# Attention and a mixture of experts on one core: the first expert's outputs, the overflow lists and their loads in another order

## The reference

```python
scores = jax.nn.softmax(x @ gate_w.T, axis=-1)
topk_w, topk_idx = jax.lax.top_k(scores, TOP_K)          # TOP_K = 6
...                                                      # C = 768 slots per expert, in order of token
g = jnp.einsum('ecd,efd->ecf', buf, w_gate)              # F = 176
u = jnp.einsum('ecd,efd->ecf', buf, w_up)
eo = jnp.einsum('ecf,edf->ecd', jax.nn.silu(g) * u, w_down)
y = jnp.zeros_like(x).at[st].add(gathered)               # gathered: eo times the token's weight
return y + _shared_swiglu(hidden_states, sh_gate, sh_up, sh_down)
```

## Time and profile before

| | |
|---|---|
| median of 3 runs | 2354.23 us (2347.09 to 2356.7) |
| the profiled execution's own time | 2333.68 us |
| its span in the profile | 2331.8 us, 38661 instructions |
| mean granted clock of TensorE | 0.978 of full speed |
| busy, PE, DVE, ACT, POOL | 2200.4, 1329.0, 1201.2, 817.6 us |
| chain that ended last | PE 84%, DVE 8%, ACT 3%, issue 3%, POOL 2%, DMA 1% |
| POOL at line 2104 | 264 instructions, 413.6 us |

### The profile page before, as it was taken

How to read it: one execution, slowest core, us unless ns; L and a number is a source line. 1 busy time by engine, 2 the same in 40 slices (tenths; PEclk the granted TensorE clock), 3 DMA queues, 4 the chain that set the end, 5 groups by cost and what they waited for, 6 DMA issues and landing times.

```text
span 2331.8 us, 38661 instructions
## 1 busy us (share of the span) xinstructions
PE 2200.4 (94%) x14776; PEld 1986.8 (85%) x14776; DVE 1329.0 (57%) x2870; ACT 1201.2 (52%) x2231; POOL 817.6 (35%) x791
## 2 busy tenths in 40 slices
PE   8999999999999999999999999998798999999970
PEld 7999998998989899898989989898687888888860
DVE  4444444545554454555545455555667887888853
ACT  4544444444444454444445444444445777777753
POOL 3111112000014400002440000261345888878785
PEclk9999999999999999999999999999899999999995
DMA  5866722122113212111322211141549988888856
GB/s 191 318 266 263 287 80 62 47 66 75 50 54 119 89 57 77 53 51 59 120 84 60 77 59 44 60 141 46 179 160 297 212 205 206 203 204 204 211 61 231
DMA packets 152705, 310.61 MB, mean 133 GB/s; under 512 B 26529, under 2 KB 88225, under 8 KB 152513
## 3 DMA queue, kind: packets, MB, share of 16 engines
q1 hardware_dynamic: 103888, 251.98, 32.1%
q0 software_dynamic: 48192, 55.68, 12.4%
q10 hardware_dynamic: 432, 0.40, 0.1%
HBM read 168.01 MB, written 149.34 MB: 136 GB/s over the span
## 4 chain that ended last, share of the span: by engine, by line
PE 84%; DVE 8%; ACT 3%; issue 3%; POOL 2%; DMA 1%; ACTq 0%; POOLq 0%; SPq 0%; DVEq 0%
PE bank L841 52%; PE bank L1201 20%; PE bank L851 7%; PE bank L1304 2%; PE bank L1214 2%; DVE ub L1705 1%; POOL y_part L2104 1%; DVE stats L2019 0%; DVE bank L1889 0%; DVE bank L1886 0%; ACT q_hi L1429 0%; ACT silu_b L1505 0%; POOL slots L2094 0%; DVE xe_lo L1956 0%; DVE ha_lo L1891 0%
## 5 line engine op out<-in xcount | busy, mean ns | idle before, releaser
L1201 PEld LDWEIGHTS bank<-v,a 128*128 128x128 f32 x4608 | 604.2, 191 | 44.1 <-ACT a L1453 0.8
L1201 PE MATMUL bank<-v,a 128*128 128x129 f32 x4608 | 617.4, 275 | 0.6 <-ACT a L1453 0.6
L2104 POOL DMA_INDIRECT y_part<-y_e,row_token x264 | 413.6, 1567 | 104.2 <-issue 84.3
L2074 POOL TENSOR_TENSOR decay_all<-decay_all,tab 128x128 f32<-128x128 f32 x128 | 60.6, 473 | 944.7 <-DMA decay_all<-decay_dram 944.4
L1449 ACT ACTIVATE a<-bank,c_s 128x512 f32<-128x512 f32 x384 | 263.0, 686 | 181.4 <-PE bank L841 167.9
L1453 ACT ACTIVATE a<-ub 128x512 f32<-128x512 f32 (+1 forms) x256 | 133.9, 524 | 379.0 <-DVE ub L1705 371.9
L2094 POOL DMA_INDIRECT slots<-rows,slot_u x192 | 189.4, 987 | 275.7 <-PE bank L1201 119.4
L841 PE MATMUL bank<-q_hi,k_hi 128*128 128x512 f32 (+1 forms) x640 | 262.5, 410 | 11.3 <-DVE ub L1705 9.6
L1684 DVE TENSOR_TENSOR q_lo<-bank,q_hi 128x512 fp32r<-128x512 f32 x128 | 88.4, 691 | 278.1 <-ACT q_hi L1429 278.1
L841 PE MATMUL bank<-q_lo,k_hi 128*128 128x512 f32 (+1 forms) x640 | 237.9, 372 | 0.0
L841 PE MATMUL bank<-q_hi,k_lo 128*128 128x512 f32 (+1 forms) x640 | 236.9, 370 | 0.0
(11 more groups left out here) (216 smaller groups left out, 4911.5 us busy)
## 6 DMA issues: line engine op xcount, KB each, us to landing
slots<-acc SPq DMA_DIRECT2D x65, 816.0 KB, 7.8
w_raw_f<-in_wffn SPq DMA_DIRECT2D x66, 624.0 KB, 5.3
xr<-slots SPq DMA_DIRECT2D x64, 544.0 KB, 5.4
decay_all<-decay_dram SPq DMA_DIRECT2D x128, 128.0 KB, 3.2
w_hi<-w_dram SPq DMA_DIRECT2D x24, 384.0 KB, 4.4
w_lo<-w_dram SPq DMA_DIRECT2D x24, 384.0 KB, 5.0
sum<-y_part SPq DMA_DIRECT2D x16, 512.0 KB, 10.6
wc_hi<-wc_dram SPq DMA_DIRECT2D x24, 256.0 KB, 2.8
```

The costliest lines, as they stand in the source:

```text
L1201: ins = e.matmul(dst[:, tt, r, :], a32[u % NA][:, r, t0:t0 + P], v[n % 3][:, s, :], start=(s == 0 and r == 0), stop=(s == 2 * g + tt), ski ...
L2074: e.tensor_tensor(arg[:, GROUP:GROUP + P], arg[:, P:GROUP], mask, ALU.add)
L2104: e.indirect_dma_start(out=y_part[part], out_offset=bass.IndirectOffsetOnAxis(ap=token, axis=0), in_=y_e[y][:, j, :], in_offset=None, boun ...
```

## The change

It has three parts, none of which changes what is computed.

1. At place 1 of the expert loop, both pairs of `down` of expert 0 stand directly in front of `gate_up(k, 1)`, behind the first third of expert 1's `gate_up`, the turn of expert 2 and the rounding of expert 3's weights. Before, they stood behind `gate_up(k, 2)`. At all other places `down` stays where it was.
2. `counted` and `jobs(0)` follow `hidden` of step 11, which is the first step with no routing work in front of it; before, they followed the whole shared stage.
3. The task `over_in`, which gathered rows and weights job by job, is split in `over_rows` and `over_weights`. All eight row gathers come first, and they no longer wait for the last `gate_up` of the shared stage; the four weight gathers still do, since their buffers lie over shared inputs.

```diff
--- before.py
+++ after.py
@@ -443,10 +443,15 @@
                     do("gate_up", k, i)
             route_some(paces[k])
             hidden(k)
+            if k == jobs_at:
+                do("counted",)
+                do("jobs", 0)
 
 
     paces = [0, 0, 1, 3, 3, 3, 3, 3, 2, 3, 2]
     assert sum(paces) == len(background)
+
+    jobs_at = len(paces)
     paces += [0] * (2 * M - len(paces))
     for m in range(M):
         if m + 1 < M:
@@ -466,8 +471,6 @@
             for part in range(3):
                 do("split_lo", m - 2, part)
     assert not background and not to_send
-    do("counted",)
-    do("jobs", 0)
 
 
     def turn(x_id):
@@ -490,8 +493,9 @@
         if x_id + 2 < E:
             do("rows_in", x_id + 2)
         if place == 0:
-            for i in range(KJ):
-                do("over_in", E + i)
+            for what in ("over_rows", "over_weights"):
+                for i in range(KJ):
+                    do(what, E + i)
         if len(after) > 2 and after[2] < E:
             do("raw_in", after[2])
 
@@ -502,6 +506,9 @@
             turn(after[0])
         if len(after) > 1:
             do("split_hi", after[1])
+        if place == 1:
+
+            down(SEQ[0], (0, 1))
         do("gate_up", k, 1)
         if len(after) > 1:
             do("split_lo", after[1], 0)
@@ -510,12 +517,12 @@
             do("split_lo", after[1], 1)
         do("gate_up", k, 2)
         do("hidden", k, 2)
-        if place:
+        if place > 1:
             down(SEQ[place - 1], (0,))
         do("hidden", k, 3)
         if len(after) > 1:
             do("split_lo", after[1], 2)
-        if place:
+        if place > 1:
             down(SEQ[place - 1], (1,))
     down(SEQ[-1], (0, 1))
     return order, spare
@@ -2121,12 +2128,15 @@
                         ap=job_w[:, q:q + 1], axis=0),
                     bounds_check=NX * P - 1, oob_is_err=True).then_inc(sem, 16)
 
-            def over_in(x_id):
+            def over_rows(x_id):
                 once.wait_ge(c_jobs, 1)
                 all_sent(once)
                 once.wait_ge(s_x1, len(PARTS))
+                fetch_rows(x_id - E, xo[x_id - E], o_moved[x_id - E])
+
+            def over_weights(x_id):
+
                 once.wait_ge(c_gu, 3 * 2 * M)
-                fetch_rows(x_id - E, xo[x_id - E], o_moved[x_id - E])
                 fetch_weights(x_id - E, w_raw_o[x_id - E], o_moved[x_id - E])
 
             def down(x_id, pair):
@@ -2143,7 +2153,7 @@
                 for j in (2 * pair, 2 * pair + 1):
                     add_rows(row_token[kept_at(x_id)][:, j:j + 1], j, PLACE[x_id] % YS, part, c_add[part])
 
-            parts = dict(acc_add=acc_add, em_mask=em_mask, x_rest=x_rest, w_rest=w_rest, wv_rest=wv_rest, wc_rest=wc_rest, route=route, scatter=scatter, over_in=over_in,
+            parts = dict(acc_add=acc_add, em_mask=em_mask, x_rest=x_rest, w_rest=w_rest, wv_rest=wv_rest, wc_rest=wc_rest, route=route, scatter=scatter, over_rows=over_rows, over_weights=over_weights,
                          experts_begin=experts_begin, down=down)
 
             e.memset(ones[:, :], 1.0).then_inc(s_ones)
```

## The result

The changed kernel took 2366.37 us (median of 7 runs, 2361.63 to 2368.26), the kernel before in the same session 2354.55 us (7 runs, 2346.07 to 2360.19): ratio 1.0043, 95% interval 1.0027 to 1.0059, some 10 to 12 us slower. Forecast was +4.6 us, to 2358.8 us.

What follows compares the result with a forecast made beforehand. The end was taken to follow expert 4's output, with DVE bounding that stretch and POOL's transfers behind it. 4.1 + 0 + 0.5 = +4.6 us on 2333.68 us, plus 20.55 us, gave 2358.8 us; range 2344 to 2370 us.

Steps and rivals of the forecast that it cites:

- The bound: Expert stage: the end follows expert 4's output, set by PE, ACT and DVE; POOL then runs almost without a break.
- POOL never regains time that it once lost: Expert stage: POOL's four transfers per expert take 7.4 us, TensorE about 7.5 us, so POOL's delays stay to the end.
- POOL pausing before expert 4 for more than before: Before expert 4's transfer: longer POOL pauses than before were named as a sign that the prediction was wrong.
- Part 1, 4.1 us: Expert 0's outputs: TensorE idles 2.8 us for a bank, DVE's product comes 4.4 us later, 4.1 us reach the end.
- The clock's 1.7 us: Behind TensorE's idle before expert 0's outputs: its clock drops to the lower level, a loss of 1.7 us.
- clock stays up: Rival at the idle at 1770 us: no clock drop, part 1 is 2.4 us, time 2357.1 us; chance 0.16.
- Part 2, 0 us: Count and first job list on DVE: the 4.8 us moved ahead of hidden steps 12 to 15 cost 0 us.
- Part 3, +0.5 us: POOL's gathers for the extra jobs: earlier weights delay expert 0's row load by 0.5 us; bounds -2.3 and +3 us.
- the weights crowd out SP's loads: Rival: expert 2's weights and rows come some 3 us late; sum 8.1 us, time 2362.3 us; chance 0.12.
- no engine waited for a load there but the first: Argument against the crowding rival: in the old profile only the first load there kept an engine waiting.
- faster, the first rows come early: Rival: expert 0's load lands in 4.1 us instead of 6.4; -0.7 us in sum, 2353.5 us; chance 0.14.
- the 20.55 us that I carried over: Whole program: the three-run median lay 20.55 us above the profiled execution; this was added unchanged to the forecast.

Runs made afterwards that it cites:

- b_gathers_9: The kernel before, with POOL's twelve gathers for the extra jobs issued at expert place 9 and not at place 0: 2342.26 us, ratio 1.0051.
- b_jobs_late: The kernel before, with DVE's job lists 1 to 3 made at places 20, 36 and 52, not 3 to 5: 2320.96 us, ratio 0.9959.
- after: The changed kernel as first timed and profiled, against the kernel before: 2366.37 us, ratio 1.0043.
- full_again: The changed kernel itself, timed and profiled again in a later session, against the kernel before: 2338.24 us, ratio 1.0038.
- full_gathers_later: The changed kernel with all twelve gathers held back until the first third of expert 0's products: 2330.05 us, 0.9996 of the kernel before.
- full_weights_later: The changed kernel with only the four weight gathers held back until the first third of expert 0's products: 2357.88 us, 1.0002 of the kernel before.
- outputs_lists: The kernel before with parts 1 and 2 only, rows and weights of the extra jobs in one piece: 2361.35 us, ratio 1.0018.

## Why the prediction was right and where it was wrong

- **The bound** (POOL's chain, entered at expert 4, fed by DVE) was right in the main: b_gathers_9, b_jobs_late, and 8.8 us at expert 4 in the profile against 8.9 at the end in the medians. "POOL never regains time that it once lost" was too strong: 15.8 us put in cost 12, and the pauses of single executions differ by 6 us. That what POOL gains earlier is given back holds only with the job lists at places 3 to 5. One sign of being wrong, POOL pausing before expert 4 for more than before, came (3.71 and 4.42 us ahead of expert 1 in after and full_again); it was badly chosen, since outputs that come late make POOL wait for them.
- **Part 1, 4.1 us**: the bank's wait came as read, 2.58 and 2.64 us for 2.8, released by DVE's subtraction. Turn to expert 4's transfer grew from 54.04 us (b_gathers_9) to 56.61 us (full_gathers_later), 2.6 us. DVE's second product of expert 1 came 3.1 us later relative to the turn, not 4.4. The clock's 1.7 us was a term that can go either way: idles of 2.58 and 2.64 us left the clock up, though they are longer than the 2.31 us that cost it, and 2.66 us in full_weights_later did not. Where it fell, it cost 1.5 us. In after the "clock stays up" rival had this term right. At the end even 2.6 us is no more than the measurement can tell (0.9996 and 1.0008).
- **Part 2, 0 us**: right. From the common matmul to the last shared `gate_up` it is 31.83 us before, 31.71 and 31.84 us in full_again and full_gathers_later.
- **Part 3, +0.5 us**: this is the step that failed. It is 6.5 us at expert 4 and 8 us of the time. Its bounds (-2.3 to +3) took in only the load of expert 0's rows, where 1.9 us were measured. That much is near what followed from the Trainium skill, "DMA: Bandwidth & Descriptors", section "Queues, rings and completion order" (a DMA engine takes turns between rings, so a late gather still takes its share): 1.4 us by it, and the trace of full_again agrees with 1.9 us more than in full_gathers_later. The rest came by the rival "the weights crowd out SP's loads", chance 0.12: ACT's copy of expert 2's weights 3.2 us late against the turn where it said some 3. In after, where no copy waited, the loss came another way: the first turn was 6.8 us late, 4.5 us of it in the last shared outputs, which no rival had. The prediction had read "no engine waited for a load there but the first" as a reason against, which is a fact of the old timing.

  I also priced parts 1 and 3 apart. Part 1 hangs TensorE on a bank that comes free through ACT's weight copy, so a late load, most of which two thirds of products (2.89 us) would have covered in the old order, became idle, and behind the longer idle the clock fell after all. That the parts alone add up to 1.0025 and the whole to 1.0038 to 1.0043 agrees with it, but the intervals don't prove it.
- **Luck**: the time came within the range because in after the clock term, which stayed away, offset a part of the missed one, and because the range reached up to 2370 us for the crowding rival. The delay at expert 4 in full_again, 8.8 us, was nearly twice the sum's 4.6.
- **The rival "faster, the first rows come early"** fell: the load took 8.0 and 7.2 us, not 4.1.
- **The level**: the 20.55 us that I carried over are, by these profiles, waits of the kind above, most of them ahead of the change, which the kernel before has too. Carrying them over was right for the sum: the first profile was of the lower level, like those from chip 4, and the medians of the higher. But where they fall differs from kernel to kernel, and in after two of them fell where nothing covers them. Whether the gathers' traffic lengthens them stays open: the three profiles with early rows and weights end the shared outputs 4.3 to 6.1 us late and the one with the weights held back 1.6 us, but these are single profiles, and no run changed the waits alone.

## What to carry to other kernels

A transfer that becomes free to start earlier is not free: look at which loads start in its new stretch, sum their bytes, and follow the second and third load behind the first, not only the one that something waits for today. Before making an engine wait on a buffer, follow that buffer's release through every queue it passes, since each wait there will be added. Where one engine issues a chain that ends the program, relieve the engine that feeds its start: here moving three job lists of some 2.6 us on DVE to later places gained 8 us, where no part of the change gained anything that these times can tell.

## What the hardware showed that was not expected

- One program ran at 2329 us in a session on chip 4 and at 2355 to 2357 us in two on chip 15. The profiles of the latter have waits of ACT, DVE and PE with releaser `remote` or `issue`, and their first turn is some 24 us later. With one session on chip 4, whether the chip or the session makes the level is open, and so is what the waits are for.
- Idle of 2.48 (outputs_lists), 2.58 (after) and 2.64 us (full_gathers_later) before expert 0's outputs left TensorE's granted clock at 1.00 for the next 3 us; 2.66 us at the same place (full_weights_later) was followed by 0.77 and 0.66, 4.67 us (full_again) by 0.53. Elsewhere 2.31 us (before) and 2.46 us (full_gathers_later) were followed by 0.52 and 0.53. The length of the idle alone does not tell. The fall cost 1.5 us at expert 4's transfer.
- A gather of weights is 1.0 us on POOL's timeline and, by the kernel's shapes, moves as much as a load of weights, 624 KB. With four of them and the last gathers of rows beside them, SP's weight loads took 14.5 us in the median (full_again), and 6.1 us with all gathers later (full_gathers_later).
